# Two pieces of strip probabilities turned in one go, the second into the rotation of the three score banks

## What is computed

```python
x = x + neighbourhood_attention(group_norm(x))   # 16 heads, softmax over 7x7 keys around each token
t = tokens(x)                                    # 3136 tokens of 128 channels
s = einsum("bhqd,bhkd->bhqk", q, k) * scale      # q, k, v from layer_norm(t); 8 heads of 16
t = t + (softmax(s) @ v) @ Wo + bo
t = t + layer_norm(t) @ w_lora.T @ W.T
```

## Time and profile before

| | us |
|---|---|
| median of 3 runs | 8890.2 (8887.18 to 8890.36) |
| the profiled execution | 8895.99 |
| its span, first to last instruction | 8893.9 |
| PE busy | 8528.5 (96%) |
| DVE busy | 7401.2 (83%) |
| ACT busy | 6567.1 (74%) |
| POOL busy | 3024.4 (34%) |

### The profile page before, as it was taken

The page is one execution under the profiler, slowest core; times in us unless marked ns, Lnnn a source line. Parts: engine busy times, 40 slices in busy tenths (PEclk is TensorE's granted clock), DMA queues, the critical chain, the costliest instruction groups (busy, mean ns, idle before and its releaser), DMA issues.

```text
span 8893.9 us, 389467 instructions
## 1 busy us (share of the span) xinstructions
PE 8528.5 (96%) x173512; PEld 4534.7 (51%) x173512; DVE 7401.2 (83%) x12442; ACT 6567.1 (74%) x13653; POOL 3024.4 (34%) x3001
## 2 busy tenths in 40 slices
PE   5789999999999999999999999999999999999998
PEld 4445554555545555455554555545555455544543
DVE  5578888888888888888888888888888888889985
ACT  2367777777777777777777777777777777777877
POOL 5514442244412444034440444304443144420000
PEclk8899999999999999999999999999999999999999
DMA  1120101201011010110102001120101200111000
GB/s 46 35 56 20 26 22 28 48 19 29 26 38 31 21 28 25 44 29 19 26 26 56 18 22 28 28 47 17 26 26 28 48 16 24 27 27 32 9 10 8
DMA packets 312022, 253.97 MB, mean 29 GB/s; under 512 B 97244, under 2 KB 303052, under 8 KB 308300
## 3 DMA queue, kind: packets, MB, share of 16 engines
q1 hardware_dynamic: 310348, 229.05, 10.7%
HBM read 136.82 MB, written 78.05 MB: 24 GB/s over the span
## 4 chain that ended last, share of the span: by engine, by line
PE 86%; DVE 6%; ACT 3%; issue 3%; POOL 2%; DMA 0%; SPq 0%; POOLq 0%; ACTq 0%; DVEq 0%
PE PS L1239 23%; PE PS L1172 23%; PE PS L1224 20%; PE PS L967 7%; PE PS L1024 5%; PE PS L1031 4%; DVE block_max L1700 3%; PE PS L1038 2%; PE PS L1016 1%; ACT PB L1455 1%; ACT tail L1373 1%; DVE NM L1578 1%; PE PS L999 1%; PE PS L1081 0%; DVE X L1630 0%
## 5 line engine op out<-in xcount | busy, mean ns | idle before, releaser
L1700 DVE TENSOR_REDUCE block_max<-PS 128x1 f32<-128x512 f32 (+1 forms) x9632 | 6126.6, 682 | 932.4 <-PE PS L1172 859.8
L1455 ACT ACTIVATE PB<-PS 128x448 f32<-128x448 f32 (+1 forms) x11200 | 5385.4, 544 | 1556.8 <-PE PS L1224 1535.9
L1224 PE MATMUL PS<-QP,KP 99*32 99x448 bf16 x43904 | 4307.2, 354 | 64.9 <-ACT PB L1455 43.5
L1172 PE MATMUL PS<-KP,QP 96*32 96x512 bf16 (+1 forms) x43904 | 3998.8, 355 | 26.4 <-issue 18.6
L1239 PE MATMUL PS<-PB,VA 128*32 128x448 f32 x22400 | 2689.0, 539 | 5.3 <-issue 4.5
L1224 PEld LDWEIGHTS PS<-QP,KP 99*32 99x32 bf16 x43904 | 1417.8, 97 | 1247.4 <-issue 471.8
L1172 PEld LDWEIGHTS PS<-KP,QP 96*32 96x32 bf16 x43904 | 1291.3, 96 | 1400.1 <-issue 532.6
L880 POOL TENSOR_TENSOR SC<-SC,NM 128x1120 f32<-128x1120 f32 x210 | 433.1, 2062 | 1633.4 <-DVE NM L1578 1633.3
L1239 PEld LDWEIGHTS PS<-PB,VA 128*32 128x32 f32 x22400 | 791.0, 110 | 377.3 <-issue 4.4
L852 POOL TENSOR_TENSOR QB<-Qn,C 128x896 f32<-128x896 f32 x392 | 666.9, 1722 | 11.8 <-ACT Qn L1310 11.8
L902 POOL CAST shift_parts<-shift 14x128 bf16<-14x128 f32 x112 | 31.5, 281 | 1747.6 <-ACT shift L1366 1747.6
(11 more groups left out here) (116 smaller groups left out, 4801.9 us busy)
## 6 DMA issues: line engine op xcount, KB each, us to landing
QP<-q_dram SPq DMA_DIRECT2D x672, 56.0 KB, 2.1
VP<-vT_padded SPq DMA_DIRECT2D x448, 70.0 KB
k_dram<-k_parts SPq DMA_DIRECT2D x56, 336.0 KB, 3.0
KP<-k_dram SPq DMA_DIRECT2D x336, 56.0 KB, 2.1
q_dram<-q_parts SPq DMA_DIRECT2D x56, 336.0 KB, 2.8
KP<-k_dram SPq DMA_DIRECT2D x48, 392.0 KB, 6.1
VA<-v_dram SPq DMA_DIRECT2D x16, 816.0 KB, 4.6
vT_padded<-SC SPq DMA_DIRECT2D x112, 112.0 KB
```

The costliest lines, as they stand in the source:

```text
L1172: ins = mm(PS[at:at + QT, bank, n * width:(n + 1) * width], QP[0:ROWS, Q_SLOTS[k % AUNITS], t:t + QT], KP[0:ROWS, g, t // BLK, keys], star ...
L1224: ins = mm(PS[k0:k0 + 32, bank, 0:BLK], KP[0:ROWSM, k // NBLK, h, c * P + k0:c * P + k0 + 32], QP[0:ROWSM, Q_SLOTS[k], h * BLK:(h + 1) * B ...
L1455: S.activation(exp_buffer(k, c)[0:n, h, :], PS[0:n, at % ST_BANKS, 0:BLK], ACT.Exp, scale=float(ADIM) ** -0.5).then_inc(exp_done, 1)
L1700: V.tensor_reduce(block_max[:, k % 2, queries.start:queries.stop, j], tile, AX.X, ALU.max).then_inc(max_read, 1)
```

## The change

The turning of pieces i and i + 1 is done at one place: i into the side bank as before, i + 1 straight behind it into the next of the three score banks. The plan fixes "turn" for the first and third piece only, so a strip's four slots have 8, 0, 6 and 0 transposes at sub 0. The rotation counts the second piece as one more reader: each later score group takes the bank behind it, and the waits are for `turned_read` where the last reader of a bank was such a copy, for `exp_done` elsewhere. ACT copies both pieces in a row before the exponential h1. The front part of the first image (four goes in a row, eight banks) stays.

```diff
-            for c in range(4):
+            for c in (0, 2):
                 self.fix(t + PERIOD + 3 + c, 0, "turn", 4 * s + c)
...
+        def score_banks(kind):
+
+            places, readers = {}, []
+            for k in range(AUNITS):
+                for c in range(CHUNKS):
+                    for h in range(GH):
+                        places[k, c, h] = len(readers)
+                        readers.append(("score", k * (GH * CHUNKS) + c * GH + h))
+                        task, i = plans[kind].taken.get((k * CHUNKS + c, 0), ("none", 0))
+                        if h == 0 and task == "turn":
+                            places[i + 1] = len(readers)
+                            readers.append(("turn", i + 1))
+            return places, readers
...
+        def score_bank(b, kind, key):
+            return (b * len(score_places["first"][1]) + score_places[kind][0][key]) % ST_BANKS
+
+        def score_bank_read(b, kind, key):
+
+            n = score_places[kind][0][key] - ST_BANKS
+            if n >= 0:
+                sort, i = score_places[kind][1][n]
+            elif b == 0:
+                return exp_done, 0
+            else:
+                sort, i = score_places["first"][1][n]
+                return exp_done, of(b, -1, AUNITS * GH * CHUNKS, i + 1)
+            if sort == "turn":
+                return turned_read, of(b, 1, 4 * STRIPS, i + 1)
+            return exp_done, of(b, 0, AUNITS * GH * CHUNKS, i + 1)
...
                         previous[0] = plan.taken[t, sub]
+                        task, i = previous[0]
+                        if task == "turn":
+                            wait(pe, *score_bank_read(b, kind, i + 1))
+                            do("turn", i + 1, score_bank(b, kind, i + 1))
...
-                    at = c * GH + h
-                    bank = (k * (GH * CHUNKS) + at) % ST_BANKS
-                    seam = 1 if k == 0 and at < 2 else 0
-                    wait(pe, exp_done, of(b, 0, AUNITS * GH * CHUNKS, k * (GH * CHUNKS) + at + 1 - ST_BANKS + seam))
+                    bank = score_bank(b, kind, (k, c, h))
+                    wait(pe, *score_bank_read(b, kind, (k, c, h)))
...
                         do(task, i, SIDE_BANK)
+                        if task == "turn":
+                            do("turn", i + 1, score_bank(b, kind, i + 1))
...
-                            S.activation(exp_buffer(k, c)[0:n, h, :], PS[0:n, at % ST_BANKS, 0:BLK], ACT.Exp,
+                            S.activation(exp_buffer(k, c)[0:n, h, :], PS[0:n, score_bank(b, kind, (k, c, h)), 0:BLK], ACT.Exp,
```

More of the change, by code:

```diff
@@ L578, in hybrid_block @@
         plans = {name: Plan(name in ("first", "middle"), name) for name in ("first", "middle", "last", "after")}
+        def score_banks(kind):
[10 more added lines that the diff above has]
+            return places, readers
+        score_places = {kind: score_banks(kind) for kind in ("first", "middle", "last")}
+        def score_bank(b, kind, key):
[12 more added lines that the diff above has]
+            return exp_done, of(b, 0, AUNITS * GH * CHUNKS, i + 1)
         ALONE_SLOTS = max(t for t, sub in alone.at) + 1
```

## The result

| us | before | after |
|---|---|---|
| median | 8890.3 (8887.2 to 8893.1, 4 runs) | 8829.3 (8826.0 to 8834.0, 4 runs) |
| the profiled execution | 8896.0 | 8834.0 |
| its span | 8893.9 | 8831.9 |

What follows compares the result with a forecast made beforehand. TensorE was taken to set the pace. Gains of 37 and 20 less losses of 11, 2 and 8 make 36 us, plus 9 for waits: 45 off 8896.0, 8851, median 8845 us; range 8820 to 8870, 8 in 10 8790 to 8886.

Steps and rivals of the forecast that it cites:

- The visit: On TensorE, each stop for transposes costs 0.24 us besides the transposes themselves; 392 fewer save 94 us.
- Rival 4: On TensorE, the second piece costs a visit of its own, nothing merges: 8939 us; chance 0.11 together with rival 3.
- The wait in D: In a strip's fourth slot, h2 waits for the third's exp h3: with nothing beside it, 1.79 against 1.69 us.
- Rival 1: ACT makes up its lag within the slot, so all 392 pairs gain: 103 us, 8787 us; chance 0.20.
- The sum over A to D: Over a strip's four turning slots in order, gains less exponential waits 36 us, plus 9: together 45 us saved.
- the classes: 392 places in second and fourth slots, sorted by work at sub 1 of the slot ahead: 37 + 20 - 11 - 2 - 8.
- waits at the visits: TensorE's waits ending with a visit, for the side product's reader: half the visits go, 9 us saved, bounds nothing and 16.
- Moved products: Ten side products an image move half a slot forward into the emptied second or fourth slots, at no cost.
- Rival 2: Waits for exponentials are half as long again to twice as long: 8874 to 8903 us, about no change; chance 0.13.
- Rival 3: ACT lags in the first slot too, exp h3 at least 1.00 us after h3 everywhere: 8941 us; 0.11 with rival 4.

Runs made afterwards that it cites:

- Experiment 2: The change, with the second piece turned behind score group h1 instead of straight behind the first: 8918.1 us, ratio 1.0033 to the kernel before.
- Experiment 5: The change, with the strip's exponential at sub 1 of the strip's fourth slot, its followers later: 8815.9 us; moved only where no product is fixed at sub 1: 8810.5.
- experiment 1: The change, with the ten moved side products an image held at their old places: 8848.1 us, ratio 0.9952 to the kernel before.
- experiment 4: The change, with the strip's exponential at sub 0 of the strip's third slot, before exponential h1, instead of sub 1: 8820.3 us, ratio 0.9921.

## Why the prediction was right, and what it missed

- **The visit.** Predicted 0.24 us, 94 us in all. Experiment 2 gave it back at 0.23 each, 89 us. The transposes of the second piece follow at 0.11, in all 392 runs. Rival 4 is out. With it goes the rule of the Trainium skill (TensorEngine Tiling (Array Packing), Instruction Overhead) as the whole account of small matmuls: the matmuls are as many as before, and experiment 2, with the same number again, takes 89 us more.
- **The wait in D.** Predicted: h2 no sooner than 0.57 us after exp h3, so 1.57 us from h3 of C where nothing stands beside it. Measured 1.54 in the strip shown. Of the 84 strips with nothing beside it 42 have 1.55 to 1.59, and the 28 with a tile more have 1.33, where the prediction's figures less the 0.22 of transposes give 1.57 and 1.36; the other 14 have 1.9 and 2.5. In B behind "var2" in A the median is 1.98, where it had 1.40 + 0.57. Experiment 5, in which that exponential is in time, brought the same stretch to the 1.23 that was read off the empty slots. Rival 1 is out.
- **The sum over A to D.** Predicted 36 us by the classes and 9 for waits at the visits. The slot means give 27 and 6, 33 together, the runs of each pair alone 33 and 24, with the moved products in them. The comparison that the forecast of 45 has to stand is the one without the moves, and there it is 42 us by the medians of experiment 1. That it comes so close is in part two errors that cancel: A and B gave 32 instead of 26, C and D 6 instead of 10. The 9 us for waits that end with a visit can't be told from them. The idle time before the transposes fell by 24 us, more than the upper bound of 16, but how much of it was saved and how much turned up elsewhere the rows don't show.
- **Moved products "at no cost of their own".** This is the step that failed: the move of the products was put at nothing, and it gave about 19 us, since half a slot more lies between "k2" and the next user of the side bank. With the pairs' 42 this is the whole distance between 45 and 61. It was to be seen in the rows of before: the early product idles for the copy of "k2".
- **Rival 2**, with the waits half as long again: no sign of it. PE waits 4.7 us for VectorE's maxima by name, as before, and strips without other work lose what was worked out. The Trainium skill (TensorEngine Tiling (Array Packing), PSUM Bottleneck) says that after a speedup of TensorE the copy out of PSUM may become the bottleneck. The trace agrees in a narrow sense only: ACT is idle a quarter of the time, yet the one late exponential in C took a third of a microsecond in strips like the one shown, and experiment 4 shows that the other place in C doesn't put it right.
- **Rival 3** needed exp h3 at 1.00 us after h3 in every pair. By the timeline it stays at 0.41 in A at the median of the strips with nothing at sub 1, and the stretch from h3 of A to h2 of B has a median of 1.23 us in them.

## What to carry to other kernels

Price a small job on TensorE by the visit and by the instruction apart: compare two visits of different length, and look for one stretch without any. Before you remove work from a slot, look at what was waited for behind its back, here an exponential that the next slot needs; the time from one group to the next is the cover, and idle time in the records shows only that part of a stop which no running matmul hides. Where a planner fills gaps by itself, list what it moves: here the moves were worth 19 us one way and 14 the other.

## What was not expected of the hardware

- A wait of 0.33 us on TensorE left 0.14 us of idle time before its row (h2 at 3870.92), too little for the view to print, since matmuls of 0.36 to 0.39 us overlap at a distance of 0.2. The 85 us of named waits for exponentials are therefore not the sum of what was lost.
- Where it waits, TensorE starts a score group 0.57 to 0.59 us after the start of the exponential it waits for: 0.57 in the kernel before and in experiment 5, 0.59 in the strip shown of the kernel after, 0.57 or 0.58 at all 42 places behind "spread" and "var2" in A there.
- A run of transposes has one longer step, the first (0.143 us against 0.109), whether the run is 2, 4, 6 or 8 long; a change of the bank in its middle adds nothing.
